# Moving two normalisations of a fused transformer kernel to ScalarE, with their biases made on GpSimd

## The chip, the cores and the metric

The kernel runs on one core of a Trainium2 chip, as one launch. A core has TensorE (PE in the profile: matmuls and transposes), VectorE (DVE), ScalarE (ACT), GpSimd (POOL) and SyncE (SP, which issues DMAs). Each works through its own list of instructions in order; between engines there are only semaphores, on which an engine waits in its list. The metric is the device time of the launch in microseconds (us), lower is better.

## The reference

Two transformer layers over 8 sequences of 512 tokens of width 128, all float32, with a LayerNorm after each of the four blocks. The change lies in the last two of them.

```python
def _layernorm(x, eps=1e-05):            # over the last axis
    return (x - mean(x)) / sqrt(var(x) + eps)

x = _layernorm(x + _L0_attn_ref(x, ...))  # linear attention, MLP
x = _layernorm(x + _L0_ffn_ref(x, ...))   # 64 experts, top 8, capacity 64; one shared expert
# second layer, attention (gated, groups of 32 tokens):
normed = layernorm(x);  v, gate, qk from silu(normed @ W)
out = gate * (quad_out + lin_out);  x = _layernorm(x + (out @ Wout + bout + x))
# second layer, 8 experts of which 2 count:
for e in range(8): out += (a_e * sigmoid(b_e) @ Wo + bo) * comb[..., e]
x = _layernorm(x + out)
```

The first line of the second layer normalises `y`, which is itself not yet normalised (the second `_layernorm` and the one inside the attention are done at once). So from one `y` with its mean and variance the kernel makes two tiles: `z`, the input of the attention, and `x2`, the residual, which is `(y - mean) * rs + bout` with `rs = (0.25 * (var + eps)) ** -0.5`, that is twice the normalised `y`. After the attention, `x3` is the normalised sum of `x2` and the attention's output.

## The kernel before

**Stages.** The first layer's attention, the router with its 64 experts, and then the class `StageC`, the whole second layer. StageC starts near 290 us of the profile and is what the change touches.

**Passes.** StageC treats one sequence (512 tokens, 4 tiles of 128) at a time, in a pipeline of three steps. `bodies` calls, for every engine, `body(eng, ur, ua, r, a, f, t)` once per pass. In one pass `f` is the sequence whose 8 experts are computed, `a = f + 1` the one in attention, `r = a + 1` the one that is summed and prepared (`y`, `z`, `x2`), and `t = f - 1` the one whose last half is written out. This text calls the pass with `a = 3` "pass 3". Passes 1 to 6 have `r`, `a` and `f`; pass 7 has no `r`; pass 0 is written apart in `first_pass` and has no `f`; after pass 7 one pass of experts alone follows.

**Units.** The expert step is 16 units `q`: two halves of the sequence by eight experts. A unit is `up` on PE (two groups of three matmuls of 512 columns, L1424 to L1426), `sig` on ACT (two sigmoids of 128x256, L1070, tile `c_sg`), `unit` on DVE (two products, L1222, tile `c_g`), and for all but the first expert of a half an add on POOL (L934, tile `c_acc`), 14 adds per sequence, numbered `i` = 0 to 13; `i` = 7 to 13 belong to units 9 to 15. There are 4 buffers `c_g`, so unit `i` on DVE waits for add `i - 4`.

**Order around the change.** Everything else is slotted between units by hand, by a table:

```python
AT = dict(zT=0, accT=(8, 1), out=(9, 2), gate=2, y4=(10, 3), quads=3, gate2=3, v=4, outb=(15, 5), kT=5, sim=6, off=7, atd=6, av=8, w=9, x3=10, x3T=12, lg=13, y=7, z=11)
```

The steps named later: after unit 9 DVE adds `x2` to the attention's output in the PSUM bank `X` (L1400) and takes its statistics `mv_a`; POOL makes `rs_a` of them (`rstd`: an add L919, a power L921); after unit 10 DVE normalises `X` into `x3` (`norm`, L1193) and then adds up the first half of the experts' output (`half_sum`, L1236 to L1250); after unit 11 ACT makes `z` (`make_z`, L1031); after unit 12 PE transposes `x3` (L1642), ACT copies the transposed tile as `x3h` (L1122), DVE takes the rest, `x3l` (L1406); at unit 13 the gate's logits follow. POOL makes `x2` in three steps (L997 subtract, L999 multiply, L1001 add `bout`) after the adds 4 to 6 and before `rs_a`; then come the adds 7 to 11, `rs_f` (L919, L921), and the adds 12 and 13.

**Who waits for POOL.** PE's own function isn't printed below; the two places in it that matter are

```python
def up(f, uf, q):                      # unit q needs the products of unit q - 2
    pe.wait_ge(freed, 16 * f + (q - 1))
def half_transposes(n, un, half):      # second half: in the next pass, after unit 1 (L1463)
    pe.wait_ge(s["acc"], 14 * n + 7 * (half + 1))
```

so the transposes of the second half need all 14 adds, and `up` of unit `q` needs DVE's unit `q - 2`.

Of the kernel before, what the change touches and what calls it, by code (L numbers as in the profile page):

```python
# [663 lines left out]
class StageC:  # L664
# [245 lines left out]
    def pool(self, pool):  # L910
# [33 lines left out]
        def body(pool, ur, ua, r=None, a=None, f=None, t=None):  # L944
# [28 lines left out]
            if r is not None:  # L973
# [8 lines left out]
                else:  # L982
# [12 lines left out]
                    at = at + 3  # L995
                g.tensor_tensor(rs, rs, k["mhalf"][:, :], ALU.pow).then_inc(s["rz_step"], 1)
                g.tensor_tensor(x2, y3d, bcast_last(mean, D), ALU.subtract).then_inc(s["rz_step"], 1)  # L997
                pool.wait_ge(s["rz_step"], at + 5)
                g.tensor_tensor(x2, x2, bcast_last(rs, D), ALU.mult).then_inc(s["rz_step"], 1)  # L999
                pool.wait_ge(s["rz_step"], at + 6)  # L1000
# [1094 lines left out]
```

## Time and profile before

| | |
|---|---|
| time, median of 3 runs | 639.04 us (635.58 to 644.13) |
| span of the profiled execution | 656.7 us |
| time of the profiled execution outside its span | not among the times shown |
| PE busy | 560.0 us (85%) |
| DVE busy | 469.3 us (71%) |
| POOL busy | 433.9 us (66%) |
| ACT busy | 304.8 us (46%) |

The profiled execution is one more run of the same program; its span, from the first to the last instruction, is 17.7 us above the median of the timed runs. Busy shares are means over stages that are limited by different things. In StageC PE, DVE and POOL are all busy most of the time, so what is waited for has to be read from one pass.

### The profile page before, as it was taken

How to read it: one execution, taken by the hardware profiler on the slowest of the kernel's cores; microseconds unless marked ns; L12 is line 12 of the kernel's file. 1: busy time of each engine (PE TensorE's matmuls, PEld its weight loads, DVE VectorE, ACT ScalarE, POOL GpSimd, SP SyncE). 2: the span in 40 equal slices, each digit the busy share in tenths (PEclk: the TensorE clock that was granted, in tenths of full speed). 3: DMA queues.
4: the chain of work that ended last, by engine and by line, in shares of the span. 5: the costliest groups of instructions: out<-in, count | busy, mean ns of one | idle time of the engine just before them, and what ended most of it. 6: DMA issues, size and time to landing. Idle time of an engine off the chain costs nothing.

```text
span 656.7 us, 10345 instructions
## 1 busy us (share of the span) xinstructions
PE 560.0 (85%) x3181; PEld 457.0 (70%) x3181; DVE 469.3 (71%) x1573; ACT 304.8 (46%) x825; POOL 433.9 (66%) x478
## 2 busy tenths in 40 slices
PE   5978888699337868888898998989989899899993
PEld 4767777555226656677687886878968789788772
DVE  1568788689949423477677879877897888887873
ACT  2657765449201111125364735646456464464440
POOL 6454443319574566538887998988889899653673
PEclk9999998989555555599999999989999999799997
DMA  4697666559320121142330030300403000000000
GB/s 129 168 330 279 244 241 247 225 137 236 76 67 28 45 61 50 34 163 106 125 129 1 12 134 8 137 1 9 137 9 116 21 10 9 0 17 1 8 9 16
DMA packets 47225, 62.04 MB, mean 94 GB/s; under 512 B 13026, under 2 KB 39873, under 8 KB 46146
## 3 DMA queue, kind: packets, MB, share of 16 engines
q1 hardware_dynamic: 44610, 56.15, 26.8%
q0 software_dynamic: 2560, 5.23, 2.8%
q8 instruction: 25, 0.41, 0.3%
q14 instruction: 30, 0.25, 0.1%
HBM read 35.16 MB, written 24.13 MB: 90 GB/s over the span
## 4 chain that ended last, share of the span: by engine, by line
PE 48%; DVE 19%; issue 5%; POOL 5%; another core or an unknown queue 3%; DMA 2%; ACT 2%; POOLq 0%; SPq 0%; DVEq 0%
PE pair L1424 8%; PE pair L1425 8%; PE pair L1426 8%; PE pair L1757 5%; PE pair L1536 2%; DVE cand L1953 2%; DVE c_g L1222 2%; PE pair L1634 2%; PE pair L1767 2%; POOL c_acc L934 2%; DVE keyT L1955 2%; PE pair L1541 2%; POOL c_rs_a L921 1%; PE pair L2063 1%
## 5 line engine op out<-in xcount | busy, mean ns | idle before, releaser
L934 POOL TENSOR_TENSOR c_acc<-c_acc,c_g 128x512 f32<-128x512 f32 x112 | 144.4, 1290 | 39.9 <-DVE c_g L1222 32.9
L1070 ACT ACTIVATE c_sg<-pair 128x256 f32<-128x256 f32 x256 | 95.4, 386 | 94.7 <-PE pair L1426 92.1
L1424 PE MATMUL pair<-c_w_hi,c_x3h 128*128 128x512 f32 x256 | 111.1, 434 | 14.1 <-DVE c_g L1222 13.1
L1222 DVE SCALAR_TENSOR_TENSOR c_g<-pair,c_comb,c_sg 128x256 f32<-128x256 f32 x224 | 100.6, 478 | 26.2 <-ACT c_sg L1070 21.1
L1426 PE MATMUL pair<-c_w_hi,c_x3l 128*128 128x512 f32 x256 | 102.7, 401 | 0.0
L1425 PE MATMUL pair<-c_w_lo,c_x3h 128*128 128x512 f32 x256 | 102.6, 401 | 0.0
L1424 PEld LDWEIGHTS pair<-c_w_hi,c_x3h 128*128 128x128 f32 x256 | 49.4, 193 | 25.7 <-DVE c_g L1222 16.0
L1426 PEld LDWEIGHTS pair<-c_w_hi,c_x3l 128*128 128x128 f32 x256 | 49.2, 192 | 11.8
L1425 PEld LDWEIGHTS pair<-c_w_lo,c_x3h 128*128 128x128 f32 x256 | 49.5, 193 | 8.2
L1835 POOL DMA_INDIRECT routed_rows<-x1T_all,dest_row x32 | 31.7, 992 | 30.6 <-DVE x1T_all L1747 21.4
L1830 POOL DMA_INDIRECT rows_all<-token_rows,tok_row x32 | 31.3, 977 | 14.8 <-issue 9.4
L2002 DVE TENSOR_TENSOR hexp<-sil,pair 96x128 f32<-96x128 f32 x32 | 9.1, 283 | 39.7 <-ACT sil L1739 29.5
L952 POOL TENSOR_TENSOR c_c<-c_c 128x2048 f32<-128x2048 f32 x7 | 32.2, 4595 | 2.1 <-DVE c_lk L1314 2.1
L1739 ACT ACTIVATE sil<-pair 96x128 f32<-96x128 f32 x32 | 8.7, 273 | 49.6 <-PE pair L1757 32.6
L1757 PEld LDWEIGHTS pair<-xgT,wgu_late 128*96 128x96 f32 x160 | 29.6, 285 | 1.4 <-ACT xgT L1930 0.7
L1747 DVE TENSOR_SCALAR x1T_all<-pair,rows_all 64x128 f32<-64x128 f32 x64 | 22.3, 349 | 10.5 <-remote 5.4
L1757 PE MATMUL pair<-xgT,wgu_late 128*96 128x64 f32 x160 | 29.1, 364 | 0.2
L1930 ACT COPY xgT<-pair 128x128 f32<-128x128 f32 x32 | 8.5, 264 | 43.9 <-PE pair L2063 27.9
L1025 ACT ACTIVATE c_sgt<-pair 128x512 f32<-128x512 f32 x40 | 23.0, 598 | 6.0 <-PE pair L1426 5.2
L1767 PE MATMUL pair<-wd_late,hexp 96*64 96x128 f32 x80 | 13.9, 448 | 11.0 <-DVE hexp L2002 8.2
L1088 ACT COPY c_accT<-pair 128x512 f32<-128x512 f32 x16 | 9.4, 587 | 27.9 <-PE pair L1463 27.5
L2063 PE MATMUL pair<-ident,rows_all 128*128 128x128 f32 x32 | 15.2, 473 | 7.3 <-DMA rows_all<-token_rows,tok_row 7.3
(374 smaller groups left out, 1478.8 us busy)
## 6 DMA issues: line engine op xcount, KB each, us to landing
routed_rows<-rows_all SPq DMA_DIRECT2D x8, 2048.0 KB
c_c<-routed_rows SPq DMA_DIRECT2D x7, 2048.0 KB, 8.2
...
```

Source lines behind the costliest of these rows:

```text
L934: g.tensor_tensor(acc, acc, b["g"][:, (2 * uf + i) % 4, :, :], ALU.add).then_inc(s["acc"], 1)
L952: g.tensor_tensor(c[:, :, 0:512], c[:, :, 0:512], c[:, :, 512:1024], ALU.add).then_inc(s["sum_step"], 1)
L1025: a_.activation(b[f"sgt{step % 2}"][:, :], src[:, :], SIG).then_inc(s["sig5"], 1)
L1070: a_.activation(b[f"sg{q % 2}"][:, x, :], self.pair[q % 2][:, x, H1:2 * H1], SIG).then_inc(s["sig"], 1)
L1222: v.scalar_tensor_tensor(out=dst, in0=self.pair[q % 2][:, x, 0:H1], scalar=b[f"comb{uf}"][:, j * E1 + e:j * E1 + e + 1], in1=b[f"sg{q % 2} ...
L1424: t.matmul(dst, w_hi, x_hi, start=start, stop=False)
L1425: t.matmul(dst, w_hi, x_lo, start=False, stop=False)
L1426: return t.matmul(dst, w_lo, x_hi, start=False, stop=stop)
L1757: ins = nc.tensor.matmul(bank[2 + m % 2][0:F0, gu * P + h * CAP:gu * P + (h + 1) * CAP], wgu[:, h, gu, :], xgT[m % 2][:, h * CAP:(h + 1) * ...
L1767: ins = nc.tensor.matmul(bank[4 + m % 2][h * CAP:(h + 1) * CAP, 0:D], hexp[m % 2][:, h * CAP:(h + 1) * CAP], wd[:, h, :], start=True, stop ...
L1830: g.indirect_dma_start(rows_all[:, m * ROW:(m + 1) * ROW], None, table, bass.IndirectOffsetOnAxis(ap=tok_row[:, m:m + 1], axis=0)).then_in ...
L1835: g.indirect_dma_start(contrib, bass.IndirectOffsetOnAxis(ap=dest_row[:, m:m + 1], axis=0), y_all[:, m * D:(m + 1) * D], None, bounds_chec ...
```

## The change

`x2` and `x3` (sequences 1 to 7) are made by ACT, each as four activations `Identity(scale * in + bias)` on 128x128 with a scale and a bias per token, as `z` is already. POOL makes the two biases, `nm_x = -mean * rs_r` and `nm_a = -mean_a * rs_a` on 128x4. The add of `bout` to `x2` stays on POOL, moves behind `nm_a`, and waits there for a new semaphore, `x2a`, that ACT raises when `x2` is scaled. DVE's `norm` of `x3` and POOL's subtract and multiply on 128x512 go.

```diff
@@ pool @@
+                    g.tensor_tensor(rs, rs, k["mhalf"][:, :], ALU.pow).then_inc(s["rz_step"], 1)
+                    g.tensor_scalar(b["nm_x"][:, :], mean, -1.0, None, ALU.mult).then_inc(s["rz_step"], 1)
+                    pool.wait_ge(s["rz_step"], at + 8)
+                    g.tensor_tensor(b["nm_x"][:, :], b["nm_x"][:, :], rs, ALU.mult).then_inc(s["rz_step"], 1)
...
+            if a is not None and not first(a):
...
+                pool.wait_ge(s["rs_step"], 3 * a + 1)
+                g.tensor_tensor(b["nm_a"][:, :], b["nm_a"][:, :], b["rs_a"][:, :], ALU.mult).then_inc(s["rs_a"], 1)
+            if r is not None and not first(r):
+                pool.wait_ge(s["x2a"], r)
                 g.tensor_tensor(x2, x2, bcast_mid(k["bout_bc"][:, :], NT), ALU.add).then_inc(s["x2"], 1)
-            if a is not None and not first(a):
-                rstd("a", a + 1, "rs_step", a + 1, "rs_a")
@@ act @@
+        def make_x2(r, ur):
+            act.wait_ge(s["rz_step"], 9 * r + 6)
+            for j in range(NT):
+                c = slice(j * D, (j + 1) * D)
+                ins = a_.activation(b[f"x2{ur}"][:, c], b["y"][:, c], ACT.Identity, scale=b["rs_r"][:, j:j + 1], bias=b["nm_x"][:, j:j + 1])
+            ins.then_inc(s["x2a"], 1)
+
+        def make_x3(a, ua):
+            act.wait_ge(s["rs_a"], a + 1)
+            for j in range(NT):
+                c = slice(j * D, (j + 1) * D)
+                ins = a_.activation(b[f"x3{ua}"][:, c], X[:, c], ACT.Identity, scale=b["rs_a"][:, j:j + 1], bias=b["nm_a"][:, j:j + 1])
+            ins.then_inc(s["x3"], 1)
...
                 if a is not None:
+                    if q == AT["x3"]:
+                        make_x3(a, ua)
...
                 if r is not None and q == AT["z"]:
                     make_z(r, ur)
+                if r is not None and q == AT["x3T"]:
+                    make_x2(r, ur)
@@ dve @@
-                if a is not None and q == AT["x3"]:
-                    dve.wait_ge(s["rs_a"], a + 1)
-                    norm("a", b[f"x3{ua}"], X, b["rs_a"], s["x3"])
```

**POOL, in a pass, from the power for `x2` to the adds.** What stands in brackets is what an instruction waits for. Before:

```order
L996 TENSOR_TENSOR c_rs_r<-c_rs_r,c_mhalf 128x4 [waits c_rz_step]
L997 TENSOR_TENSOR c_x<-c_y,c_mv_r 128x512
L999 TENSOR_TENSOR c_x<-c_x,c_rs_r 128x512 [waits c_rz_step]
L1001 TENSOR_TENSOR c_x<-c_x,c_bout_bc 128x512 [waits c_rz_step]
L919 TENSOR_TENSOR c_rs_a<-c_mv_a,c_eps 128x4 [waits c_mv_a]
L921 TENSOR_TENSOR c_rs_a<-c_rs_a,c_mhalf 128x4 [waits c_rs_step]
L934 TENSOR_TENSOR c_acc<-c_acc,c_g 128x512 [waits c_g]
L934 TENSOR_TENSOR c_acc<-c_acc,c_g 128x512 [waits c_acc,c_g] x4
```

The same place after:

```order
L995 TENSOR_TENSOR c_rs_r<-c_rs_r,c_mhalf 128x4 [waits c_rz_step]
L996 TENSOR_SCALAR c_nm_x<-c_mv_r 128x4
L998 TENSOR_TENSOR c_nm_x<-c_nm_x,c_rs_r 128x4 [waits c_rz_step]
L1009 TENSOR_TENSOR c_rs_a<-c_mv_a,c_eps 128x4 [waits c_mv_a]
L1010 TENSOR_SCALAR c_nm_a<-c_mv_a 128x4
L1012 TENSOR_TENSOR c_rs_a<-c_rs_a,c_mhalf 128x4 [waits c_rs_step]
L1014 TENSOR_TENSOR c_nm_a<-c_nm_a,c_rs_a 128x4 [waits c_rs_step]
L1017 TENSOR_TENSOR c_x<-c_x,c_bout_bc 128x512 [waits c_x2a]
L934 TENSOR_TENSOR c_acc<-c_acc,c_g 128x512 [waits c_g]
L934 TENSOR_TENSOR c_acc<-c_acc,c_g 128x512 [waits c_acc,c_g] x4
```

The add of `bout` moved from before `rs_a` to behind it, and stands between `rs_a` and the adds 7 to 11 with a wait on ACT.

**ACT, in a pass, from the sigmoids of unit 10 to those of unit 13.** Before:

```order
L1070 ACTIVATE c_sg<-pair 128x256 [waits c_g,c_u_mm]
L1070 ACTIVATE c_sg<-pair 128x256 [waits c_g0,c_u_mm]
L1070 ACTIVATE c_sg<-pair 128x256 [waits c_g,c_u_mm]
L1031 ACTIVATE c_z<-c_y,c_nm,c_rq 128x128 [waits c_rz_step]
L1031 ACTIVATE c_z<-c_y,c_nm,c_rq 128x128 x3
L1070 ACTIVATE c_sg<-pair 128x256 [waits c_g0,c_u_mm]
L1070 ACTIVATE c_sg<-pair 128x256 [waits c_g,c_u_mm]
L1122 CAST c_x3h<-pair 127x512 [waits c_x3T_mm]
L1070 ACTIVATE c_sg<-pair 128x256 [waits c_g0,c_u_mm]
```

The same place after:

```order
L1099 ACTIVATE c_sg<-pair 128x256 [waits c_g,c_u_mm]
L1059 ACTIVATE c_x<-pair,c_nm_a,c_rs_a 128x128 [waits c_rs_a]
L1059 ACTIVATE c_x<-pair,c_nm_a,c_rs_a 128x128 x3
L1099 ACTIVATE c_sg<-pair 128x256 [waits c_g0,c_u_mm]
L1099 ACTIVATE c_sg<-pair 128x256 [waits c_g,c_u_mm]
L1045 ACTIVATE c_z<-c_y,c_nm,c_rq 128x128 [waits c_rz_step]
L1045 ACTIVATE c_z<-c_y,c_nm,c_rq 128x128 x3
L1099 ACTIVATE c_sg<-pair 128x256 [waits c_g0,c_u_mm]
L1099 ACTIVATE c_sg<-pair 128x256 [waits c_g,c_u_mm]
L1153 CAST c_x3h<-pair 127x512 [waits c_x3T_mm]
L1052 ACTIVATE c_x<-c_y,c_nm_x,c_rs_r 128x128 [waits c_rz_step]
L1052 ACTIVATE c_x<-c_y,c_nm_x,c_rs_r 128x128 x3
```

Four activations for `x3` came in ahead of the sigmoids of unit 11, with a wait on `rs_a`, and four for `x2` behind `x3h`, ahead of the sigmoids of unit 13.

## Rows read from the trace of the kernel before

**Rows 1.** The page, chain that ended last: shares of the span by engine.

```profile
PE 48%; DVE 19%; issue 5%; POOL 5%; another core or an unknown queue 3%; DMA 2%; ACT 2%; POOLq 0%; SPq 0%; DVEq 0%
```

**Rows 2.** Chain of waits, 300 to 657 us: start, length, engine, tile, line.

```profile
350.94 1.03 POOL c_rs_a L921
...
392.12 1.03 POOL c_rs_a L921
...
433.19 1.03 POOL c_rs_a L921
...
477.13 1.03 POOL c_rs_a L921
...
559.56 1.03 POOL c_rs_a L921
...
603.34 1.03 POOL c_rs_a L921
```

**Rows 3.** Timeline of PE, pass 4: start, length, idle time before in brackets.

```profile
479.61 0.66 PE L1642 MATMUL pair<-ident,c_x 128*128 128x128 f32 x4
482.00 0.50 PE L1424 MATMUL pair<-c_w_hi,c_x3h 128*128 128x512 f32 x1 [1.74 <-DVE c_g L1222]
...
490.96 0.63 PE L1463 MATMUL pair<-ident,c_acc 128*128 128x128 f32 x4
```

**Rows 4.** Timeline of DVE, pass 4.

```profile
478.18 1.37 DVE L1193 TENSOR_SCALAR c_x<-pair,c_mv_a,c_rs_a 128x128 f32<-128x128 f32 x4 [0.33 <-POOL c_rs_a L921]
479.47 0.17 DVE L1236 TENSOR_REDUCE c_csum<-c_comb 128x4 f32<-128x32 f32 x1
...
481.49 1.63 DVE L1222 SCALAR_TENSOR_TENSOR c_g<-pair,c_comb,c_sg 128x256 f32<-128x256 f32 x4
```

**Rows 5.** Timeline of POOL, pass 4.

```profile
475.20 1.29 POOL L1001 TENSOR_TENSOR c_x<-c_x,c_bout_bc 128x512 f32<-128x512 f32 x1
476.85 0.20 POOL L919 TENSOR_TENSOR c_rs_a<-c_mv_a,c_eps 128x4 f32<-128x4 f32 x1 [0.36 <-DVE c_mv_a L1146]
477.13 1.02 POOL L921 TENSOR_TENSOR c_rs_a<-c_rs_a,c_mhalf 128x4 f32<-128x4 f32 x1
478.12 2.70 POOL L934 TENSOR_TENSOR c_acc<-c_acc,c_g 128x512 f32<-128x512 f32 x2
482.42 4.15 POOL L934 TENSOR_TENSOR c_acc<-c_acc,c_g 128x512 f32<-128x512 f32 x3 [1.60 <-DVE c_g L1222]
486.51 0.20 POOL L919 TENSOR_TENSOR c_rs_f<-c_mv_f,c_eps 128x2 f32<-128x2 f32 x1
...
487.48 1.28 POOL L934 TENSOR_TENSOR c_acc<-c_acc,c_g 128x512 f32<-128x512 f32 x1
489.39 1.29 POOL L934 TENSOR_TENSOR c_acc<-c_acc,c_g 128x512 f32<-128x512 f32 x1 [0.63 <-DVE c_g L1222]
```

**Rows 6.** Timeline of ACT, pass 4.

```profile
478.35 0.39 ACT L1070 ACTIVATE c_sg<-pair 128x256 f32<-128x256 f32 x1 [0.32 <-PE pair L1426]
478.63 1.64 ACT L1031 ACTIVATE c_z<-c_y,c_nm,c_rq 128x128 f32<-128x128 f32 x4
480.17 0.63 ACT L1070 ACTIVATE c_sg<-pair 128x256 f32<-128x256 f32 x2
480.69 0.58 ACT L1122 CAST c_x3h<-pair 127x512 fp32r<-127x512 f32 x1
483.00 0.39 ACT L1070 ACTIVATE c_sg<-pair 128x256 f32<-128x256 f32 x1 [1.73 <-PE pair L1426]
```

**Rows 7.** Line L934, 612 to 645 us: count, shortest/median/longest in ns.

```profile
L934 POOL TENSOR_TENSOR c_acc<-c_acc,c_g x17: 1260/1290/1311, 611.5 to 644.0; 128x512 f32<-128x512 f32 x17
```

**Rows 8.** Windows: stretch, us, busy of PE, PEld, DVE, ACT, POOL, granted PE clock, DMA.

```profile
394.00:397.00 3.00, 1.26 (x9) 0.64 (x7) 2.84 (x15) 2.27 (x7) 1.67 (x2) 1.00 0.00 0
436.00:439.00 3.00, 1.26 (x7) 0.89 (x6) 2.88 (x13) 1.28 (x4) 1.41 (x2) 1.00 0.00 0
439.00:442.00 3.00, 3.00 (x13) 2.55 (x12) 1.89 (x6) 0.77 (x2) 2.71 (x3) 0.51 0.00 0
```

More of the change, by code:

```diff
@@ L714, in buffers @@
             k(f"st_{n}", [P, 6 * NT]); k(f"mv_{n}", [P, 2 * NT]); k(f"rs_{n}", [P, NT])
-        k("rq", [P, NT]); k("nm", [P, NT])
+        k("rq", [P, NT]); k("nm", [P, NT]); k("nm_x", [P, NT]); k("nm_a", [P, NT])
         for n in ("top", "dif", "s1", "s2", "zap"):
@@ L721, in buffers @@
         self.s = {n: self.sem("c_" + n) for n in """pad w1_mm w1_hi w1_lo first_sum sum_step y st_r mv_r rz_step z zT_mm zh zl lin
-            v_mm gate_mm x2 sig5 prod5 quads diag_mm t1 t2 atd kT_mm kT kv_mm state0 state av_mm go w_mm y3 st_a mv_a rs_step rf_step rs_a x3
+            v_mm gate_mm x2 sig5 prod5 quads diag_mm t1 t2 atd kT_mm kT kv_mm state0 state av_mm go w_mm x2a y3 st_a mv_a rs_step rf_step rs_a x3
             x3T_mm x3h x3l lg_mm gate_step sig_d u_mm sig g0 g acc accT_mm accT out_mm bo4 st_f mv_f rs_f outb ml""".split()}
@@ L994, in body @@
                     pool.wait_ge(s["rz_step"], at + 6)
[L995 to L1000, printed above, removed]
+                    g.tensor_tensor(rs, rs, k["mhalf"][:, :], ALU.pow).then_inc(s["rz_step"], 1)
@@ new lines, in body @@
+                    g.tensor_scalar(b["nm_x"][:, :], mean, -1.0, None, ALU.mult).then_inc(s["rz_step"], 1)
+                    pool.wait_ge(s["rz_step"], at + 8)
+                    g.tensor_tensor(b["nm_x"][:, :], b["nm_x"][:, :], rs, ALU.mult).then_inc(s["rz_step"], 1)
+                if first(r):
+                    g.tensor_tensor(rs, rs, k["mhalf"][:, :], ALU.pow).then_inc(s["rz_step"], 1)
+                    g.tensor_tensor(x2, y3d, bcast_last(mean, D), ALU.subtract).then_inc(s["rz_step"], 1)
+                    pool.wait_ge(s["rz_step"], at + 5)
+                    g.tensor_tensor(x2, x2, bcast_last(rs, D), ALU.mult).then_inc(s["rz_step"], 1)
+                    pool.wait_ge(s["rz_step"], at + 6)
+                    g.tensor_tensor(x2, x2, bcast_mid(k["bout_bc"][:, :], NT), ALU.add).then_inc(s["x2"], 1)
@@ new lines, in body @@
+            if a is not None and not first(a):
+                mean_a = b["mv_a"][:, :].rearrange("p (j t) -> p j t", t=2)[:, :, 0]
+                pool.wait_ge(s["mv_a"], a + 1)
+                g.tensor_tensor(b["rs_a"][:, :], b["mv_a"][:, :].rearrange("p (j t) -> p j t", t=2)[:, :, 1], k["eps"][:, :], ALU.add).then_inc(s["rs_step"], 1)
+                g.tensor_scalar(b["nm_a"][:, :], mean_a, -1.0, None, ALU.mult).then_inc(s["rs_step"], 1)
+                pool.wait_ge(s["rs_step"], 3 * a - 1)
+                g.tensor_tensor(b["rs_a"][:, :], b["rs_a"][:, :], k["mhalf"][:, :], ALU.pow).then_inc(s["rs_step"], 1)
+                pool.wait_ge(s["rs_step"], 3 * a + 1)
+                g.tensor_tensor(b["nm_a"][:, :], b["nm_a"][:, :], b["rs_a"][:, :], ALU.mult).then_inc(s["rs_a"], 1)
@@ L1128, in body @@
                     make_z(r, ur)
+                if r is not None and q == AT["x3T"]:
+                    make_x2(r, ur)
         self.bodies(act, body)
```

## The prediction

> **What bounds the kernel now.** I read the page's chain first: PE carries the largest share of it [rows 1]. Then the chain of waits in order of time, for one step that every pass has, POOL's power for `rs_a` [rows 2]. It tells the length of a pass: 392.12 - 350.94 = 41.18 us. Six passes lie between the first and the last of these rows, 603.34 - 350.94 = 252.40 us, and two of them are longer: 477.13 - 433.19 = 43.94 and 603.34 - 559.56 = 43.78. Last I read pass 4 engine by engine. There PE works without a gap but for one: after the transposes of `x3` (479.61, 0.66 us) it stands 1.74 us until DVE's unit 11 is done [rows 3]. DVE is late there because it first normalises `x3` (1.37 us) and then sums the experts' half from 479.47 to 481.49 [rows 4]. So PE bounds a pass, with one gap for which DVE and POOL's `rs_a` are to blame. ACT has room in the pass as a whole.
>
> The reader should look at POOL next, since the change adds its wait there. From the moment `mv_a` is there (476.85) POOL has `rs_a`, seven adds and `rs_f` to do, with gaps of only 1.60 and 0.63 us, and ends at 489.39 + 1.29 = 490.68 [rows 5]. PE's transposes of the second half, which need all fourteen adds, start at 490.96 [rows 3]. POOL is therefore as near to the path as PE: it has 1.60 + 0.63 = 2.23 us to give in this stretch, and behind it nothing.
>
> **The two longer passes.** In pass 3 the granted clock is 1.00 up to 439 and 0.51 after it, the lower of the two levels (1.2 GHz), behind a stretch in which PE was busy 1.26 of 3 us; in pass 2 a stretch of the same 1.26 us left the clock at 1.00 [rows 8]. A fall of this kind costs 43.94 - 41.18 = 2.76 and 2.60 us, together 5.4 us of this execution.
>
> **The change, on pass 4's time line.** All steps up to `mv_a` at 476.85 stay as they are, as nothing they need moves: POOL leaves out the subtract and the multiply before it (475.20 is the start of the third step), but POOL waited for `mv_a` anyway, 0.36 us [rows 5]. What is removed there is idle time afterwards. `x2` itself is first needed a pass later.
>
> Step 1, the bias. POOL puts two more instructions on 128x4 into the way of `x3`. Such an instruction takes 477.13 - 476.85 = 0.28 us with its hand-over [rows 5], so scale and bias are there not at 477.13 + 1.02 = 478.15 but at about 478.71, and ACT starts at 478.75.
>
> Step 2, ACT. The block of four activations with scale and bias takes 1.64 us, and the next instruction starts 480.17 - 478.63 = 1.54 us after it; a pair of sigmoids takes 480.69 - 480.17 = 0.52; `x3h` 0.58, with overlap 0.55 [rows 6]. `x3` is done at 478.75 + 1.64 = 480.39, against 478.18 + 1.37 = 479.55 on DVE before [rows 4]: 0.8 us later. In the list of ACT follow the sigmoids 11 (from 480.29), `z` (480.81), the sigmoids 12 (482.35), `x3h` (482.87; the transposes of `x3` are done at about 481.1, so it doesn't wait), and `x2` (483.42 to 485.06). The sigmoids of unit 13 come behind that, at 484.96 instead of 483.00 [rows 6].
>
> `x3` reads PSUM with scale and bias per token, which the trace doesn't show on ACT. The block's own numbers say that one activation takes 0.485 us and the next starts 0.385 after it (three starts and one length make 1.64, four starts 1.54). Above, without overlap, a block is 4 x 0.485 = 1.94; below, at the pace of the sigmoids (0.26 each, from PSUM, twice as wide), 1.04 us. I take 1.54 to 1.64, the same form on the same size. Two new blocks per pass make that -1.0 to +0.8 us per pass.
>
> Step 3, PE's gap. DVE, rid of the norm, does `half_sum` while ACT makes `x3`, and unit 11 follows its first sigmoid (480.29 + 0.39 = 480.68) at 480.7, against 481.49 [rows 4]. PE's gap before unit 13 ends at 481.2 instead of 482.00 [rows 3]. That is the gain that the change has, 0.8 us, and in passes 1 to 6 it isn't kept:
>
> Step 4, POOL's wait. Behind `nm_a` (478.71) POOL waits for `x2a` till 485.1, 6.4 us in which it did two adds before. Queued behind the waiting instruction are the add of `bout` (1.29), the adds 7 to 11, `rs_f`, and the adds 12 and 13. An add costs 4.15 / 3 = 1.38, `rs_f` 487.48 - 486.51 = 0.97 [rows 5]. The end: 485.1 + 1.29 + 7 x 1.38 + 0.97 = 497.0, with no gap left inside, against 490.68. Waiting for it: DVE's unit 13 for add 7 (485.1 + 1.29 + 1.38 = 487.8), unit 14 and 15 behind it; PE's `up` of unit 15 for that; the first half's output for `rs_f` (494.3); and at last PE's transposes at L1463 for add 13, 497.3 instead of 490.96. In between PE has the work of 490.96 - 479.61 - 1.74 = 9.6 us [rows 3] for some 17 us; I estimate that 3 us of its standing come just before L1463, since the units ahead of it have their products 1 to 4 us before add 13 is done. **The price is 6.3 us in each of the passes 1 to 6.** Behind L1463 both POOL and PE are late by the same 6.3 us, so the rest of the pass runs as before, and up to the next `mv_a` nothing catches up: PE has no gaps there.
>
> So a pass takes 41.18 + 6.3 = 47.5 us, at either clock before 497, as PE has time for the lower level there. Six of them: 285.0, against 252.40 measured with the two falls: +32.6. Pass 7 has no `x2`, hence no wait; it keeps step 3, -0.8. In pass 0 `x2` stands on ACT before the gate's sigmoids, while these wait for DVE, and POOL comes back to its next sum about 1 us later, where the adds had to wait longer than that: 0.
>
> Step 5, the clock behind the wait. PE resumes at 497.3 from a longer gap than the 1.74 us that led to a fall twice in seven. Of falls inside the stalled stretch nothing is felt; one that comes at its end costs 2.7 each. Between 0 and 6 of them, 0 to 16 us; I take two, +5.4, the number that the profile had.
>
> Sum: 32.6 - 0.8 + 5.4 = +37.2 us. The profiled execution's own time isn't known beyond its span of 656.7, which would become 694. It lies 17.7 us above the median, so I add the difference as it is: 639.04 + 37 = **676 us**, 5.8% slower.
>
> **A rule against the trace.** The adds of step 4 run while DVE stands. The seventeen adds of the last passes, where DVE is loaded unevenly and POOL often waits for it, take between 1260 and 1311 ns [rows 7], so I give an add the same length whatever DVE does. The Trainium skill, GPSIMD Engine Reference, section Key points, says that GpSimd shares its SBUF interfaces with VectorE and contends with some of its instructions. By that rule the adds would be shorter beside an idle DVE and the sum smaller; the rows give at most 30 ns for it, 7 x 0.03 = 0.2 us per pass.
>
> **Rivals.** *The wait is hidden (not slower).* If POOL's wait cost nothing, step 3 would be kept in seven passes, 7 x 0.8 = 5.6, and with gaps of 0.9 instead of 1.74 us (0.8 before the transposes of `x3`, 0.1 behind) the falls might go, 5.4: 639 - 11 = 628. Place: POOL before the add of `bout`. It decides from the point where `x2a` comes by 490.68 - 11.9 = 478.8; in ACT's list `x2` stands behind `x3`, which itself starts at 478.75. Against it speaks the order; for it, only that the adds or the 2.2 us of gaps hold more than I read. 5%.
>
> *Half of it is hidden.* The adds take up part of the delay, or the blocks on ACT run at the lower bound (-1.0 per pass) and `z` or `x3h` cost less beside them: 3 to 4.5 us per pass, +12 to +21 net, 651 to 660. 11%.
>
> *The clock falls behind every wait.* Same mechanism, but PE resumes at the lower level in five or six passes: 32.6 - 0.8 + 6 x 2.7 = +48, 687. For it: PE has only those 9.6 us of work in the 17 us ahead of it. Against: at the lower level the same matmuls fill most of that time, so PE isn't idle for long, and the clock came back by itself in the passes before. 20%.
>
> **How the numbers follow.** The forecast, POOL's wait with 0 to 3 falls, 671 to 679, and some us for the blocks on ACT: 64%. The range takes in the rival with all falls and its upper block cost (687 + 4), and half of the one that is partly hidden: 655 to 692. The three runs spread over 1.3%, so 2% is about what a measurement can tell from no change. Faster by more than that needs under 626, less than the hidden wait gives: 3%. Within 2% (626 to 652): most of the hidden wait and a part of the half-hidden one, 7%. Slower: 90%.
>
> **What would show it.** In the profile after, POOL's add of `bout` idles about 6.4 us in passes 1 to 6, with ACT's `x2` as its releaser; that wait isn't there before. The pass, read at POOL's power for `rs_a`, is 47.5 us. DVE's unit 13 and PE's L1463 have idle time with POOL's `c_acc` as releaser, and the chain of waits has POOL's adds where it had PE. In pass 7 PE has 0.8 us idle before the transposes of `x3` and nearly none behind them. ACT's blocks for `x3` take 1.6 us. I am wrong if POOL's wait is under 3 us, if an add runs much faster than 1.29 us beside a standing DVE, or if the end of a pass has slack that I didn't see, so that PE starts L1463 before add 13's shift reaches it.

## The result, and the profile after

The changed kernel takes 672.22 us in the median (670.29 to 673.08, 4 runs), the kernel before 640.64 us beside it (635.58 to 644.13, 4 runs). The ratio is 1.0547, 95% interval 1.0503 to 1.0591: 5.5% slower. It leaves disturbed runs out and so is not the quotient of the two medians. The profiled run of the changed kernel took 671.81 us, its span is 670.1, so 1.7 us lie outside.

The page of the changed kernel: busy time of the engines (part 1), the chain that ended last (part 4), and the group of POOL's add of `bout` (part 5: count, busy, mean ns, idle time before it and who ended it).

```profile
PE 574.1 (86%) x3181; PEld 465.5 (69%) x3181; DVE 462.0 (69%) x1545; ACT 322.4 (48%) x881; POOL 424.3 (63%) x492
...
PE 37%; DVE 17%; POOL 15%; ACT 5%; issue 5%; DMA 2%; POOLq 0%; SPq 0%; DVEq 0%; ACTq 0%
...
L934 POOL TENSOR_TENSOR c_acc<-c_acc,c_g 128x512 f32<-128x512 f32 x112 | 143.9, 1285 | 22.2 <-DVE c_g L1255 13.3
...
L1017 POOL TENSOR_TENSOR c_x<-c_x,c_bout_bc 128x512 f32<-128x512 f32 x7 | 9.0, 1290 | 40.0 <-ACT c_x L1052 40.0
```

POOL is *less* busy than before (424.3 against 433.9 us), DVE too (462.0 against 469.3), and yet POOL's share of the chain went from 5% [rows 1] to 15%. What it has on the path is no more work, but a wait, and the adds queued behind it. The table of waits, StageC (330 to 671 us), columns: who waits for whom, us in total, times, longest:

```profile
POOL c_x L1017 <- ACT c_x L1052: 37.4, 6, 6.2
...
DVE c_g L1255 <- POOL c_acc L934: 20.0, 6, 3.3
...
PE pair L1493 <- POOL c_acc L934: 14.1, 8, 2.8
...
PE pair L1586 <- DVE c_x3l L1436: 8.4, 6, 1.4
```

The first row is the cause, six waits of 6.2 us, one per pass (experiments 1 to 3 test it); the second and third are how it reaches PE. The fourth is new too and isn't part of that chain.

The chain of waits, from 290 us on, POOL's power for `rs_a` (start, length), which answers to [rows 2]:

```profile
332.83 1.01 POOL c_rs_a L1012
...
379.92 1.01 POOL c_rs_a L1012
...
428.44 1.01 POOL c_rs_a L1012
...
475.78 1.01 POOL c_rs_a L1012
...
522.74 1.01 POOL c_rs_a L1012
...
571.34 1.01 POOL c_rs_a L1012
...
618.29 1.00 POOL c_rs_a L1012
```

The six passes take 47.1, 48.5, 47.3, 47.0, 48.6 and 47.0 us, together 285.46, against 252.40 [rows 2]: +33.06. From the last of these rows to the end of the span it is 670.1 - 618.29 = 51.8 us, before 656.7 - 603.34 = 53.4: -1.5. That makes +31.5, and the medians differ by 31.6. All of the loss lies in passes 1 to 6. (The spans can't be subtracted from each other: the profiled execution of before was 18 us longer ahead of StageC's first `rs_a`, in code that the change doesn't touch.)

Pass 4 of the changed kernel answers to [rows 3 to 6]. The timeline of POOL (start, length, and in brackets the idle time before):

```profile
475.75 1.04 POOL L1012 TENSOR_TENSOR c_rs_a<-c_rs_a,c_mhalf 128x4 f32<-128x4 f32 x1
476.86 0.20 POOL L1014 TENSOR_TENSOR c_nm_a<-c_nm_a,c_rs_a 128x4 f32<-128x4 f32 x1
483.30 1.29 POOL L1017 TENSOR_TENSOR c_x<-c_x,c_bout_bc 128x512 f32<-128x512 f32 x1 [6.24 <-ACT c_x L1052]
484.55 6.96 POOL L934 TENSOR_TENSOR c_acc<-c_acc,c_g 128x512 f32<-128x512 f32 x5
...
492.42 2.69 POOL L934 TENSOR_TENSOR c_acc<-c_acc,c_g 128x512 f32<-128x512 f32 x2
```

The timeline of ACT in the same pass:

```profile
477.10 1.51 ACT L1059 ACTIVATE c_x<-pair,c_nm_a,c_rs_a 128x128 f32<-128x128 f32 x4 [1.21 <-POOL c_nm_a L1014]
478.48 0.67 ACT L1099 ACTIVATE c_sg<-pair 128x256 f32<-128x256 f32 x2
479.00 1.67 ACT L1045 ACTIVATE c_z<-c_y,c_nm,c_rq 128x128 f32<-128x128 f32 x4
480.55 0.68 ACT L1099 ACTIVATE c_sg<-pair 128x256 f32<-128x256 f32 x2
481.07 0.62 ACT L1153 CAST c_x3h<-pair 127x512 fp32r<-127x512 f32 x1
481.54 1.69 ACT L1052 ACTIVATE c_x<-c_y,c_nm_x,c_rs_r 128x128 f32<-128x128 f32 x4
```

The timeline of PE, the five places where it waits:

```profile
478.66 0.66 PE L1672 MATMUL pair<-ident,c_x 128*128 128x128 f32 x4 [0.39 <-ACT c_x L1059]
479.52 0.50 PE L1454 MATMUL pair<-c_w_hi,c_x3h 128*128 128x512 f32 x1 [0.21 <-DVE c_g L1255]
...
482.58 0.28 PE L1586 MATMUL pair<-c_wg_hl,c_x3h 128*128 128x16 f32 x1 [1.39 <-DVE c_x3l L1436]
...
486.39 0.79 PE L1454 MATMUL pair<-c_w_hi,c_x3h 128*128 128x512 f32 x1 [1.01 <-DVE c_g L1255]
...
495.17 0.66 PE L1493 MATMUL pair<-ident,c_acc 128*128 128x128 f32 x4 [1.56 <-POOL c_acc L934]
```

The timeline of DVE, its unit 13:

```profile
485.85 0.88 DVE L1255 SCALAR_TENSOR_TENSOR c_g<-pair,c_comb,c_sg 128x256 f32<-128x256 f32 x2 [3.33 <-POOL c_acc L934]
```

Read across: ACT ends `x2` at 483.23, POOL's `bout` starts at 483.30, and the adds 7 to 11, which used to start at once behind `rs_a` [rows 5], start at 484.55. DVE's unit 13 needs the buffer that add 7 frees, so it starts at 485.85, and PE's transposes of the second half start at 495.17, 19.4 us behind `rs_a`'s power; before it was 490.96 - 477.13 = 13.8 [rows 3, 5].

### The profile page after: what moved, and what is told of

Its sections match the earlier page's. It is cut to its first block, busy times and chain, and to the rows that moved or that the text cites. A ratio compares the mean times of both kernels' runs of the same rounds, so it can differ in the third digit from the quotient of the medians.

```text
span 670.1 us, 10387 instructions
## 1 busy us (share of the span) xinstructions
PE 574.1 (86%) x3181; PEld 465.5 (69%) x3181; DVE 462.0 (69%) x1545; ACT 322.4 (48%) x881; POOL 424.3 (63%) x492
## 4 chain that ended last, share of the span: by engine, by line
PE 37%; DVE 17%; POOL 15%; ACT 5%; issue 5%; DMA 2%; POOLq 0%; SPq 0%; DVEq 0%; ACTq 0%
POOL c_acc L934 10%; PE pair L1454 6%; PE pair L1455 6%; PE pair L1456 6%; PE pair L1787 4%; DVE cand L1983 3%; DVE keyT L1985 3%; PE pair L1566 2%; PE pair L1797 2%; PE pair L1664 2%; PE pair L1571 2%; ACT c_x L1052 1%; PE pair L1493 1%; ACT c_sg L1099 1%; PE pair L2093 1%
## 5 line engine op out<-in xcount | busy, mean ns | idle before, releaser
L934 POOL TENSOR_TENSOR c_acc<-c_acc,c_g 128x512 f32<-128x512 f32 x112 | 143.9, 1285 | 22.2 <-DVE c_g L1255 13.3
L1099 ACT ACTIVATE c_sg<-pair 128x256 f32<-128x256 f32 x256 | 92.7, 389 | 77.2 <-PE pair L1456 75.0
L1454 PE MATMUL pair<-c_w_hi,c_x3h 128*128 128x512 f32 x256 | 115.3, 450 | 10.8 <-DVE c_g L1255 9.8
L1456 PE MATMUL pair<-c_w_hi,c_x3l 128*128 128x512 f32 x256 | 105.9, 414 | 0.0
L1455 PE MATMUL pair<-c_w_lo,c_x3h 128*128 128x512 f32 x256 | 105.8, 413 | 0.0
L1456 PEld LDWEIGHTS pair<-c_w_hi,c_x3l 128*128 128x128 f32 x256 | 51.2, 200 | 12.5
L1455 PEld LDWEIGHTS pair<-c_w_lo,c_x3h 128*128 128x128 f32 x256 | 51.3, 201 | 8.0
L1017 POOL TENSOR_TENSOR c_x<-c_x,c_bout_bc 128x512 f32<-128x512 f32 x7 | 9.0, 1290 | 40.0 <-ACT c_x L1052 40.0
L1769 ACT ACTIVATE sil<-pair 96x128 f32<-96x128 f32 x32 | 8.7, 273 | 31.6 <-PE pair L1787 31.6
```

The source lines that it names most:

```text
L934: g.tensor_tensor(acc, acc, b["g"][:, (2 * uf + i) % 4, :, :], ALU.add).then_inc(s["acc"], 1)
L1099: a_.activation(b[f"sg{q % 2}"][:, x, :], self.pair[q % 2][:, x, H1:2 * H1], SIG).then_inc(s["sig"], 1)
L1454: t.matmul(dst, w_hi, x_hi, start=start, stop=False)
L1455: t.matmul(dst, w_hi, x_lo, start=False, stop=False)
L1456: return t.matmul(dst, w_lo, x_hi, start=False, stop=stop)
```

## The experiments

Ten kernels were run, one of them twice. The first four shared a chip, with a median of 638.47 us for the kernel before; the fifth to seventh another (651.84), the eighth and ninth a third (654.87), the last two a fourth (637.92). So only ratios are compared between them. The diffs are against the changed kernel where nothing else is said. "Pass" is always the distance of POOL's powers for `rs_a` in the timeline of POOL, passes 1 to 6.

**1. Take POOL's wait off the adds' way, everything else as changed.**

```diff
-            if r is not None and not first(r):
-                pool.wait_ge(s["x2a"], r)
-                g.tensor_tensor(x2, x2, bcast_mid(k["bout_bc"][:, :], NT), ALU.add).then_inc(s["x2"], 1)
             if f is not None:
                 add_experts(f, uf, 7, 8, 9, 10, 11)
                 rstd_f(f, 0)
                 add_experts(f, uf, 12, 13)
+            if r is not None and not first(r):
+                pool.wait_ge(s["x2a"], r)
+                g.tensor_tensor(x2, x2, bcast_mid(k["bout_bc"][:, :], NT), ALU.add).then_inc(s["x2"], 1)
```

> The changed kernel, but POOL's add of bout with its wait for x2a stands behind the adds 12 and 13, at the end of the pass, where x2a has long come. My theory (POOL's wait for x2a costs some 6 us in each of the passes 1 to 6): most of the loss goes. A pass falls from 47.1 to about 42.2 us, not to 41.2, since the sigmoids of unit 13 stay behind x2 on ACT, about 1.3 us late, and the add of bout now delays the next sum: time 645 to 650 us. Rival (the longer list of ACT is what costs, POOL's wait only shows it): the pass stays above 45 us and the time above 660 us.

Measured: 639.85 us (637.75 to 642.04, 10 runs), ratio 1.0031 (1.0000 to 1.0063); passes 42.14, 42.83, 42.15, 42.84, 42.14, 42.84. The timeline of POOL in pass 4 of this kernel:

```profile
459.03 2.71 POOL L934 TENSOR_TENSOR c_acc<-c_acc,c_g 128x512 f32<-128x512 f32 x2
...
472.36 1.30 POOL L1021 TENSOR_TENSOR c_x<-c_x,c_bout_bc 128x512 f32<-128x512 f32 x1
```

The add of `bout` has no bracket: by the time POOL comes to it `x2` has long been made. Moving these three lines gives back all of the 5.5% but 0.3%. The loss was the place of a wait and not the work on ACT. The pass came out as expected and the time lower: I had counted from a pass of before without a fall of the clock, but before has two falls of the granted clock, 5.4 us of its time, where three passes here are only 0.7 us longer than the others. A pass of 42.14 us is still 1.0 longer than one of before; the expectation put that down to the sigmoids of unit 13 behind `x2`, and kernel 2, where they aren't, has 41.3.

**2. Leave POOL's list and move ACT's `x2` ahead, to unit 9.**

```diff
-                if r is not None and q == AT["x3T"]:
+                if r is not None and q == 9:
                     make_x2(r, ur)
```

> The changed kernel, but ACT makes x2 after unit 9, where it stood idle for 3 us in each pass; POOL's add of bout stays behind nm_a and finds x2a raised. My theory: POOL's wait is gone (idle before the add of bout under 0.3 us), its 1.29 us fit into the gaps of 2.2 us that POOL had, and ACT's sigmoids of unit 13 come as early as before. What stays is z ahead of x3h on ACT behind x3, about 0.25 us per pass: time 636 to 643 us, the same as before the change. Rival (the two small instructions and ACT's slower x3 cost by themselves): 648 us or more.

Measured: 636.08 us (632.8 to 639.3, 12 runs), ratio 0.9972 (0.9940 to 1.0004); passes 42.95, 41.33, 42.94, 41.27, 41.43, 41.31. The timeline of POOL in pass 4:

```profile
457.07 1.29 POOL L1017 TENSOR_TENSOR c_x<-c_x,c_bout_bc 128x512 f32<-128x512 f32 x1
```

POOL's `bout` follows `nm_a` without idle time. The same wait goes, this time from its other end. Both repairs agree, and time and passes are as expected.

**3. Make the suspected wait longer.** ACT makes the four activations of `x2` twice in passes 1 to 6, the first time into a tile that nobody reads:

```diff
             act.wait_ge(s["rz_step"], 9 * r + 6)
+            if r > 1:
+                act.wait_ge(s["x2a"], r - 1)
+                for j in range(NT):
+                    c = slice(j * D, (j + 1) * D)
+                    a_.activation(b["dump"][:, c], b["y"][:, c], ACT.Identity, scale=b["rs_r"][:, j:j + 1], bias=b["nm_x"][:, j:j + 1])
             for j in range(NT):
```

> The changed kernel, with ACT's block of four activations for x2 doubled (the first four write a tile that nobody reads) in the passes 1 to 6. My theory: ACT's block lies on the path to POOL's add of bout, so each pass grows by the block's 1.54 us, six times: +9.2 us, 681 us; the idle time of POOL before the add of bout grows from 6.2 to 7.8 us. Rival (the loss is somewhere else, and between x2 and DVE's unit 13 there is slack): the time stays at 672 us within 2.

Measured: 681.98 us (681.31 to 682.16, 4 runs), ratio 1.0696 (1.0630 to 1.0762); passes 48.55, 48.45, 48.85, 48.42, 48.56, 49.95. The timeline of POOL, pass 4:

```profile
490.55 1.27 POOL L1017 TENSOR_TENSOR c_x<-c_x,c_bout_bc 128x512 f32<-128x512 f32 x1 [7.77 <-ACT c_x L1057]
```

POOL's wait grows from 6.24 to 7.77 us in each of the six passes. Four passes of the changed kernel took 47.1 in the mean and take 48.4 to 50.0 here; the shortest is 1.5 us longer than the shortest there, which is what ACT's `x2` takes longer. The other two, which a fall of the clock had made 48.5 and 48.6, stay at that; the falls lie elsewhere in them. Together the six grow from 285.46 to 293.28 us, by 7.8 where 6 x 1.54 = 9.2 was expected. That the time is nevertheless the 681 us expected is in part luck: the first `rs_a` of this profile comes 2.8 us later (299.85 against 297.06), ahead of everything that the edit touches.

**4. `x3` alone on ACT** (before, with `nm_a` on POOL and `make_x3`; `x2` stays on POOL in three steps).

```diff
-                    g.tensor_scalar(b["nm_x"][:, :], mean, -1.0, None, ALU.mult).then_inc(s["rz_step"], 1)
...
+                g.tensor_tensor(x2, y3d, bcast_last(mean, D), ALU.subtract).then_inc(s["rz_step"], 1)
...
+                g.tensor_tensor(x2, x2, bcast_last(rs, D), ALU.mult).then_inc(s["rz_step"], 1)
...
-                if r is not None and q == AT["x3T"]:
-                    make_x2(r, ur)
```

> The kernel before, with x3 alone moved to ACT and nm_a made by POOL; x2 stays on POOL as it was. By step 3 of the prediction PE's gap before unit 13 shrinks by 0.8 us in seven passes, and the falls of the clock behind it may go: 629 to 636 us. Rival (the gap only moves: the trace of the changed kernel shows PE idle 1.4 us before the logits, because x3h now comes behind z on ACT): the logits start no earlier than before, a pass keeps 41.2 to 41.5 us, time 637 to 643 us.

Measured: 635.80 us (633.06 to 640.13, 12 runs), ratio 1.0015 (0.9976 to 1.0054); passes 42.95, 41.28, 41.42, 42.86, 41.40, 41.30. PE's gaps in pass 4:

```profile
461.34 0.66 PE L1655 MATMUL pair<-ident,c_x 128*128 128x128 f32 x4 [0.40 <-ACT c_x L1045]
462.20 0.50 PE L1437 MATMUL pair<-c_w_hi,c_x3h 128*128 128x512 f32 x1 [0.21 <-DVE c_g L1238]
465.25 0.28 PE L1569 MATMUL pair<-c_wg_hl,c_x3h 128*128 128x16 f32 x1 [1.39 <-DVE c_x3l L1419]
```

The rival came true: the ratio is that of no change, and the passes are the 41.2 to 41.5 us that the rival gave, but for two with a fall. The one gap of 1.74 us [rows 3] became three that sum to 2.00. The gain of my step 3 is given back some 3 us later, before the gate's logits: they need `x3l`, that needs `x3h`, and on ACT `x3h` stands behind `z`, which `x3` pushed back by 1.5 us.

**5. `x2` and `z` both ahead, at unit 9.**

```diff
-AT = dict(zT=0, accT=(8, 1), out=(9, 2), gate=2, y4=(10, 3), quads=3, gate2=3, v=4, outb=(15, 5), kT=5, sim=6, off=7, atd=6, av=8, w=9, x3=10, x3T=12, lg=13, y=7, z=11)
+AT = dict(zT=0, accT=(8, 1), out=(9, 2), gate=2, y4=(10, 3), quads=3, gate2=3, v=4, outb=(15, 5), kT=5, sim=6, off=7, atd=6, av=8, w=9, x3=10, x3T=12, lg=13, y=7, z=9)
...
-                if r is not None and q == AT["x3T"]:
+                if r is not None and q == 9:
                     make_x2(r, ur)
```

> The changed kernel, but ACT makes both z and x2 after unit 9. My theory: behind x3 only the sigmoids of units 11 and 12 then stand ahead of x3h, so x3h comes 1.5 us earlier, the logits some 0.9 us earlier than in the kernel before, and what is left of the gain on DVE is kept: a pass of 40.3 us without a fall of the clock, 631 to 636 us, faster than before by about 1%. Rival (PE and POOL are bound elsewhere in the pass, so that an earlier x3l buys nothing): 41.2 us per pass, the time of e2_x2_early.

Measured: 644.16 us (640.86 to 650.53, 12 runs), ratio 0.9906 (0.9871 to 0.9942); passes 40.84, 40.69, 41.12, 40.70, 40.87, 40.70. A pass is 0.4 to 0.8 us longer than the 40.3 expected. With `z` out of the way the gap before the logits is gone, but PE waits for the adds once more, in pass 3 (timeline of PE):

```profile
442.39 0.66 PE L1493 MATMUL pair<-ident,c_acc 128*128 128x128 f32 x4 [0.80 <-POOL c_acc L934]
```

The adds are late because the add of `bout` stands directly ahead of them, as the timeline of POOL shows for the same pass:

```profile
430.14 1.29 POOL L1017 TENSOR_TENSOR c_x<-c_x,c_bout_bc 128x512 f32<-128x512 f32 x1
431.38 5.59 POOL L934 TENSOR_TENSOR c_acc<-c_acc,c_g 128x512 f32<-128x512 f32 x4
```

Kernel 8 bears this out: it has the same order on ACT and `bout` elsewhere, and PE doesn't wait for these adds there.

**6. `x2` alone on ACT, at the place of the change**, `x3` on DVE as before:

```diff
-                mean_a = b["mv_a"][:, :].rearrange("p (j t) -> p j t", t=2)[:, :, 0]
...
+                rstd("a", a + 1, "rs_step", a + 1, "rs_a")
...
-                    if q == AT["x3"]:
-                        make_x3(a, ua)
...
+                if a is not None and q == AT["x3"]:
+                    dve.wait_ge(s["rs_a"], a + 1)
+                    norm("a", b[f"x3{ua}"], X, b["rs_a"], s["x3"])
```

> The kernel before with x2 alone moved to ACT, at the changed kernel's place, and POOL's wait for x2a behind rs_a; x3 stays on DVE. My theory: x2a comes 1.5 us plus 0.6 us earlier than in the changed kernel, since x3 isn't ahead of it on ACT, so the wait is 4.7 us instead of 6.2 and a pass 45.2 instead of 47.0 us: 658 to 664 us. Rival (the loss needs both moves, since ACT is overfull only with both): within 1% of the kernel before.

Measured: 679.80 us (678.53 to 682.13, 4 runs), ratio 1.0459 (1.0399 to 1.0518); passes 46.71, 45.07, 46.98, 45.07, 46.71, 45.08. The timeline of POOL:

```profile
490.97 1.29 POOL L1010 TENSOR_TENSOR c_x<-c_x,c_bout_bc 128x512 f32<-128x512 f32 x1 [4.75 <-ACT c_x L1045]
```

Wait and pass came as expected (4.7 and 45.2), the time higher, as three passes are 1.6 to 1.9 us longer by a fall. So `x2` with its wait costs 45.1 - 41.2 = 3.9 us a pass, `x3` alone nearly nothing (41.3), both together 5.9: `x3` stands ahead of `x2` on ACT, and counts in full once POOL waits for `x2`. The add of `bout` starts 483.30 - 475.75 = 7.55 us behind the power for `rs_a` in the changed kernel and 490.97 - 485.20 = 5.77 here, 1.8 us apart, of which `x3`'s block is 1.5.

**7. `x3` on ACT, `x2` on POOL, and `z` at unit 9** (kernel 4 with one more number):

```diff
-AT = dict(zT=0, accT=(8, 1), out=(9, 2), gate=2, y4=(10, 3), quads=3, gate2=3, v=4, outb=(15, 5), kT=5, sim=6, off=7, atd=6, av=8, w=9, x3=10, x3T=12, lg=13, y=7, z=11)
+AT = dict(zT=0, accT=(8, 1), out=(9, 2), gate=2, y4=(10, 3), quads=3, gate2=3, v=4, outb=(15, 5), kT=5, sim=6, off=7, atd=6, av=8, w=9, x3=10, x3T=12, lg=13, y=7, z=9)
```

> The kernel before with x3 alone on ACT, and z after unit 9; x2 stays on POOL. If z ahead of x3h is what ate the gain of step 3, a pass is 40.3 us and the time that of e5_x2_z_early, 631 to 636 us. If moving x2 off POOL is needed for it (POOL is near the path), it is slower than e5 by more than 2 us.

Measured: 639.86 us (637.27 to 642.18, 6 runs), ratio 0.9840 (0.9794 to 0.9886); passes 40.11, 40.03, 40.11, 40.02, 40.11, 40.02. PE's only gaps are 0.40 to 0.48 before the transposes of `x3` and 0.20 behind them. The pass is 0.2 us shorter than expected, and moving `x2` off POOL isn't needed for it. Here step 3 is real, 41.18 - 40.07 = 1.1 us a pass.

**8. Kernel 5 with the add of `bout` and its wait ahead of `rs_a`**, where the kernel before has it:

```diff
+            if r is not None and not first(r):
+                pool.wait_ge(s["x2a"], r)
+                g.tensor_tensor(x2, x2, bcast_mid(k["bout_bc"][:, :], NT), ALU.add).then_inc(s["x2"], 1)
             if a is not None and not first(a):
                 mean_a = b["mv_a"][:, :].rearrange("p (j t) -> p j t", t=2)[:, :, 0]
```

> The kernel e5_x2_z_early with POOL's add of bout, and its wait for x2a, ahead of rs_a, where POOL stands for 3 us. In e5 a pass is 40.7 us with PE waiting 0.5 to 0.8 us for POOL's add 13; in e7, with x2 on POOL and finished before rs_a, it is 40.05. My theory (the 1.29 us between nm_a and add 7 are on the path once PE is faster): a pass of 40.0 to 40.1 us, ratio to the kernel before 0.982 to 0.986, like e7. Rival (ACT's extra four activations ahead of the sigmoids of unit 10 cost it): it stays at 40.7 us.

Measured: 648.44 us (645.74 to 652.57, 12 runs), ratio 0.9930 (0.9895 to 0.9966); passes 40.96, 40.82, 40.93, 40.85, 40.94, 40.00. The expectation failed. The timeline of POOL:

```profile
466.02 0.20 POOL L998 TENSOR_TENSOR c_nm_x<-c_nm_x,c_rs_r 128x4 f32<-128x4 f32 x1
469.06 1.31 POOL L1008 TENSOR_TENSOR c_x<-c_x,c_bout_bc 128x512 f32<-128x512 f32 x1 [2.84 <-ACT c_x L1052]
```

The timeline of PE in the same pass:

```profile
473.58 0.66 PE L1672 MATMUL pair<-ident,c_x 128*128 128x128 f32 x4 [1.22 <-ACT c_x L1059]
```

POOL waits again for ACT, 2.84 us, now ahead of `rs_a`, and `rs_a` and with it `x3` come 0.8 us late: PE's gap before the transposes is 1.22 instead of 0.40. Its wait for the adds behind `rs_a`, 0.80 in kernel 5, is gone. In the sixth pass, whose 40.00 us lie behind the last `x2`, there is no such wait. Moving a wait is only good where nothing urgent is queued behind it.

**9. `z` at unit 9 alone**, an edit of one line in the kernel before:

```diff
-AT = dict(zT=0, accT=(8, 1), out=(9, 2), gate=2, y4=(10, 3), quads=3, gate2=3, v=4, outb=(15, 5), kT=5, sim=6, off=7, atd=6, av=8, w=9, x3=10, x3T=12, lg=13, y=7, z=11)
+AT = dict(zT=0, accT=(8, 1), out=(9, 2), gate=2, y4=(10, 3), quads=3, gate2=3, v=4, outb=(15, 5), kT=5, sim=6, off=7, atd=6, av=8, w=9, x3=10, x3T=12, lg=13, y=7, z=9)
```

> The kernel before with one number changed: z after unit 9 instead of unit 11; x3 and x2 stay where they were. My theory: DVE's norm of x3 and the half sum still set the products of unit 11 and x3l, so PE's gap of 1.74 us stays and a pass is 41.1 to 41.3 us: ratio 0.995 to 1.003. Rival (moving z is what makes e7 faster, and x3 on ACT adds nothing): 40.1 us per pass, ratio 0.984.

Measured: 654.43 us (650.37 to 657.41, 12 runs), ratio 1.0021 (0.9983 to 1.0058); passes 41.17, 41.06, 41.17, 41.22, 41.15, 43.75. `z`'s place is worth nothing by itself. Kernel 7's gain needs both parts: `x3` off DVE, and `x3h` not behind `z`.

**10. All of the change, with both repairs**: kernel 1 with `z` at unit 9. **11. Kernel 7 once more**, beside it.

```diff
-AT = dict(zT=0, accT=(8, 1), out=(9, 2), gate=2, y4=(10, 3), quads=3, gate2=3, v=4, outb=(15, 5), kT=5, sim=6, off=7, atd=6, av=8, w=9, x3=10, x3T=12, lg=13, y=7, z=11)
+AT = dict(zT=0, accT=(8, 1), out=(9, 2), gate=2, y4=(10, 3), quads=3, gate2=3, v=4, outb=(15, 5), kT=5, sim=6, off=7, atd=6, av=8, w=9, x3=10, x3T=12, lg=13, y=7, z=9)
```

> The changed kernel with both repairs: z at unit 9, x2 left where it is on ScalarE (behind the sigmoids of unit 12), and POOL's wait for x2a with the add of bout behind the last two adds. Theory (all of the loss is the place of POOL's wait, all of the gain is x3's place and z's): the wait is hidden, since x2 is done before POOL comes to it, and POOL's rs_a is delayed by nothing, so the pass is 40.0 to 40.1 us as in the kernel with x3 and z alone, and the ratio to the kernel before 0.982 to 0.986; x2 on ScalarE then adds no gain of its own. Rival: POOL, rid of two instructions of 1.04 us, gives the pass something back and it is under 39.9 us. Second rival: the add of bout behind the adds 12 and 13 pushes the rest of POOL's list (the output's halves) late, and the pass is 40.5 us or more.

> x3 on ScalarE and z at unit 9 once more (x2 on POOL as before), on the same chip as the kernel with both repairs, so that the two can be compared. Expected as measured before: pass 40.0 to 40.1 us, ratio 0.982 to 0.986. If the ratio comes out above 0.99, the gain seen before was one of the chip or of its session.

Measured: kernel 10 630.14 us (626.32 to 633.68, 11 runs), ratio 0.9908 (0.9872 to 0.9943), passes 40.61, 40.50, 40.62, 40.53, 40.63, 40.47. Kernel 7 again 626.27 us (624.62 to 629.02, 6 runs), ratio 0.9839 (0.9792 to 0.9886), passes 40.12, 40.02, 40.13, 40.05, 40.11, 40.07: the gain holds on another chip. The expectation for kernel 10 failed: it lies 0.5 us a pass above kernel 7, a size that I had put down for the second rival (POOL's list pushed late by the add of `bout`), but its place is another. Kernel 10 first, the timeline of DVE:

```profile
457.46 0.88 DVE L1255 SCALAR_TENSOR_TENSOR c_g<-pair,c_comb,c_sg 128x256 f32<-128x256 f32 x2 [0.85 <-ACT c_sg L1099]
```

and that of PE:

```profile
464.12 0.65 PE L1493 MATMUL pair<-ident,c_acc 128*128 128x128 f32 x4
```

In the second run of kernel 7, the timeline of DVE:

```profile
458.55 0.97 DVE L1238 SCALAR_TENSOR_TENSOR c_g<-pair,c_comb,c_sg 128x256 f32<-128x256 f32 x2
```

and that of PE:

```profile
465.72 0.60 PE L1476 MATMUL pair<-ident,c_acc 128*128 128x128 f32 x4
```

Against their `rs_a` (451.12 and 453.14) PE's transposes come at 13.00 and 12.58 us. In kernel 10 the sigmoids of unit 13 stand behind `x2`'s block on ACT, DVE stands 0.85 us for them, and that is before POOL has come to `bout`. PE shows no idle time for it, only 39.7 us busy in a pass where kernel 7 has 39.3, so that this stand of DVE is what makes the 0.4 us is argued from the order and not tested. What POOL saved, two steps of 1.04 us, only lengthens its wait for `mv_a`, from 0.2 to 2.5 us. So `x2` on ACT is worth less than nothing here, even without any wait on POOL.

## Why the prediction was right, and where its numbers were off

The sign, the mechanism and its place were right. 676 was predicted, 672.22 measured. Made against the traces the forecast was +37.2 us and the change +31.5; the 5.7 us between them are three terms, worked out below: 2.5 in the price of the wait, 2.5 in the clock, 0.7 behind the last `rs_a`. That 676 lies only 3.8 us off has some luck in it: it started from 639.04 us, and the kernel before took 640.64 beside the changed one.

**Steps 1 and 2, bias and ACT's order: right.** ACT starts `x3` 477.10 - 475.75 = 1.35 us behind the power for `rs_a`, where I had 478.75 - 477.13 = 1.62. From there everything stands in the order I had read. `x3` takes 1.51 us and `x2` 1.69, between my bounds of 1.04 and 1.94 and near the value that I took. `x2` is done 7.5 us behind the power, 0.4 less than predicted, for the most part by that start.

**Step 3, PE's gap: wrong in passes 1 to 6.** I said that unit 13 would start 0.8 us earlier and that this was "the gain that the change has", lost only because of POOL's wait. Unit 13 does start earlier, 479.52 - 475.75 = 3.8 us behind the power against 4.9 [rows 3, 5], but PE then stands 1.39 us before the logits, in kernel 4 too, where POOL waits for nothing. I had `z` ahead of `x3h` in step 2's list with its time, 482.87, and didn't ask who waits for `x3h`. The error cost nothing in the sum, since step 4 covers it, but without step 4 it would have: the "wait is hidden" rival, at 628, counted on a gain in seven passes and no falls, and kernels 1 and 2, which hide the wait, ran at 1.003 and 0.997. In pass 7, where there is no `z`, the gain is there: unit 13 starts 3.76 us behind the power and not 4.87 (the kernel before has it at 608.21), 1.1 us against the 0.8 predicted. The other 0.4 of the 1.5 us come at the very end of the span and are no part of step 3.

**Step 4, POOL's wait: right, its price 0.4 too high.** Six waits of 6.24 us were read as "about 6.4", with DVE and PE waiting for `c_acc` where I had said. Kernels 1 and 2 take the wait away from either end and the loss goes; kernel 3 lengthens it by 1.5 us, and the shortest pass grows by 1.5; kernel 6 has the wait without `x3` and pays 3.9 us. The passes without a fall behind the wait take 47.09 us in the mean (47.09, 47.34, 46.96, 46.95), not 47.5: six times 0.41 is 2.5 us.

The adds behind the wait run at 6.96 / 5 = 1.39 us each, the pace of before [rows 5]. All 112 of them take 1285 ns in the mean, against 1260 to 1311 before [rows 7], and the first behind each wait, which in pass 4 lies wholly inside the 3.33 us that DVE stands, takes 1267 to 1284: at most 0.02 us less than the 1.29 that I had used. The Trainium skill, GPSIMD Engine Reference, section Key points, says that the two engines share their SBUF interfaces and contend when VectorE runs in a 2-port mode or reads two SBUF inputs. DVE's products read one tile from PSUM and one from SBUF, so by its words the rule need not reach them; the rows leave it at most 0.02 us per add, no more than I had allowed it.

**Step 5, the clock: the number of felt falls right, the size of one wrong.** I took two falls felt at 2.7 us. The trace has a fall in every pass from 1 to 6, and two of the six are felt. Windows of the changed kernel (stretch, us, busy of PE, PEld, DVE, ACT and POOL, granted PE clock, DMA), first in pass 2, then in pass 4:

```profile
399.00:400.00 1.00, 0.70 (x4) 0.70 (x5) 0.54 (x2) 0.00 (x0) 1.00 (x2) 0.69 0.00 0
...
402.00:403.00 1.00, 1.00 (x4) 0.77 (x3) 0.48 (x1) 0.11 (x2) 1.00 (x1) 0.60 0.00 0
403.00:404.00 1.00, 1.00 (x6) 0.82 (x5) 0.48 (x1) 0.69 (x2) 1.00 (x2) 1.00 0.00 0
...
485.00:488.00 3.00, 1.99 (x5) 1.32 (x5) 1.96 (x16) 0.43 (x3) 2.71 (x3) 0.50 0.00 0
488.00:491.00 3.00, 3.00 (x9) 2.28 (x8) 2.90 (x15) 1.48 (x5) 2.71 (x3) 0.50 0.00 0
...
494.00:497.00 3.00, 1.83 (x10) 1.61 (x11) 1.37 (x3) 1.00 (x3) 3.00 (x2) 1.00 0.14 44
```

At 485 to 491, in pass 4, PE runs at the lower level while POOL is still late with its adds; the clock is back before the transposes wait for the last of them, and that pass is one of the shortest, 46.96 us. Passes 1, 3 and 6 have the same, each with some 6.8 us at the lower level. This is what step 5 said of falls inside the stalled stretch, and in part what I held against the third rival: the slower matmuls fill the stall, and PE then waits only 1.55 to 2.05 us for add 13. In passes 2 and 5 it waits 2.74 and 2.76 us, and the fall comes just behind that, where PE has been released and has no one to wait for; these passes take 48.5 and 48.6, 1.5 us above the mean of the others and not 2.7. Why the two kinds of pass take turns as they do stays open.

The size of 2.7 us came from pass 3 of before, and there the lower level lasts longer. It begins at 439 [rows 8] and ends between 445 and 446:

```profile
445.00:446.00 1.00, 1.00 (x4) 0.74 (x4) 0.97 (x4) 0.21 (x1) 0.51 (x1) 0.56 0.00 0
446.00:447.00 1.00, 1.00 (x6) 0.82 (x5) 0.88 (x5) 0.56 (x2) 0.78 (x1) 1.00 0.00 0
```

Those are some 6.8 us at the lower level, where pass 2 of the changed kernel has 3.4 (the windows from 399 to 403 have 0.69, 0.50, 0.50 and 0.60), with PE busy in both. So the term is 2.9 us instead of 5.4: the count of two felt falls, taken over from before, came out by luck, and the size of one was taken from a fall of twice the length. The rival with a fall felt behind every wait didn't come about.

**The chances.** Slower by over 2%, at 90%, came true, and the hidden and half-hidden waits are excluded by the traces. That no slack at the end of a pass takes up the delay was read from one pair of rows, add 13 ending at 490.68 and PE's transposes at 490.96 [rows 3, 5]; this was what the forecast stood on.
